# Forming the convolved half of a Mamba block's input projection directly as channels x time

## The reference

```python
xz = layernorm(x) @ in_proj_w.T          # 512 -> 2048
xi, z = split(xz, 2)                     # 1024 each
xt = conv1d(transpose(xi), conv_w, 4 taps, causal, per channel) + conv_b
xc = silu(transpose(xt))                 # 1024 channels
xp = xc @ x_proj_w.T                     # dt, B, C  (33 columns)
delta = softplus(xp[..., 0:1] * dt_w + dt_b)
# for each of 16 states s: A_bar, chunked cumulative sums over 128 steps,
# y = sum_s C_s * h_s + D * xc
x = x + (y * silu(z)) @ out_proj_w.T
x = x + int8-like product of layernorm(x) with L0_ffn_rhs
```

## Time and profile before

| | |
|---|---|
| timed runs | 5839.98, 5842.17, 5845.01 us (median 5842.17) |
| the profiled execution: from its first to its last instruction | 5836.6 us (no time of its own is listed beside this span) |
| PE busy | 5616.2 us, 96% |
| DVE busy | 5351.4 us, 92% |
| ACT busy | 3734.7 us, 64% |
| POOL busy | 2457.2 us, 42% |
| granted TensorE clock, mean | 0.992 of 2.4 GHz |

### The profile page before, as it was taken

The page is one execution under the profiler, slowest core; times in us unless marked ns, Lnnn a source line. Parts: engine busy times, 40 slices in busy tenths (PEclk is TensorE's granted clock), DMA queues, the critical chain, the costliest instruction groups (busy, mean ns, idle before and its releaser), DMA issues. The chain is left out here.

```text
span 5836.6 us, 78230 instructions
## 1 busy us (share of the span) xinstructions
PE 5616.2 (96%) x16088; PEld 2643.7 (45%) x16152; DVE 5351.4 (92%) x7057; ACT 3734.7 (64%) x4618; POOL 2457.2 (42%) x2139
## 2 busy tenths in 40 slices
PE   5999999999999999999999999999999999999998
PEld 2444444444444444444444444444444444444443
DVE  4999999999999999999999999999999999999997
ACT  3666666666666666666666666666666666666664
POOL 2444444444444444444444444444444444444443
PEclk9999999999999999999999999999999999999999
DMA  1122121121121211212212112112122121121220
GB/s 68 12 18 20 15 18 16 15 20 16 15 19 14 18 17 15 20 16 15 20 14 17 17 17 18 16 15 20 14 17 19 14 18 16 15 20 16 15 18 12
DMA packets 157893, 104.23 MB, mean 18 GB/s; under 512 B 121008, under 2 KB 121008, under 8 KB 157488
## 3 DMA queue, kind: packets, MB, share of 16 engines
q1 hardware_dynamic: 157488, 100.71, 19.0%
HBM read 42.63 MB, written 16.78 MB: 10 GB/s over the span
## 5 line engine op out<-in xcount | busy, mean ns | idle before, releaser
L487 POOL TENSOR_SCALAR room<-total,limit 128x1024 f32<-128x1024 f32 x1024 | 1183.1, 1155 | 3245.6 <-PE cum L1038 475.3
L739 ACT ACTIVATE decay<-cum,neg_a 128x1024 f32<-128x1024 f32 x1024 | 1137.3, 1111 | 1543.0 <-PE cum L1038 1539.3
L1048 PE MATMUL state<-sources,tri_upto 128*128 128x512 f32 x4096 | 1971.5, 604 | 123.9 <-DVE term L1380 123.5
L1038 PE MATMUL cum<-step,tri_before 128*128 128x512 f32 x4096 | 1938.8, 596 | 3.5 <-DVE sources L1367 3.5
L1380 DVE SCALAR_TENSOR_TENSOR term<-state,crow,decay 128x1024 f32<-128x1024 f32 x1024 | 1312.6, 1282 | 312.9 <-PE state L1048 196.0
L1390 DVE TENSOR_TENSOR acc<-acc,term 128x1024 f32<-128x1024 f32 x1024 | 1359.2, 1327 | 0.2
L1367 DVE SCALAR_TENSOR_TENSOR sources<-cum,brow,dx 128x1024 f32<-128x1024 f32 x1024 | 1305.5, 1275 | 10.0 <-ACT cum L755 10.0
L1038 PEld LDWEIGHTS cum<-step,tri_before 128*128 128x128 f32 x4096 | 781.1, 192 | 966.3 <-issue 943.7
L755 ACT ACTIVATE cum<-room,pos_a 128x1024 f32<-128x1024 f32 x1024 | 1143.6, 1117 | 110.6 <-POOL room L487 101.8
L1048 PEld LDWEIGHTS state<-sources,tri_upto 128*128 128x128 f32 x4096 | 743.3, 190 | 994.3 <-issue 867.3
L476 POOL TENSOR_SCALAR step<-delta,limit 128x1024 f32<-128x1024 f32 x1024 | 1144.7, 1118 | 8.3 <-PE cum L1038 7.0
(11 more groups left out here) (127 smaller groups left out, 3630.5 us busy)
## 6 DMA issues: line engine op xcount, KB each, us to landing
hfirst<-hrows SPq DMA_DIRECT2D x496, 64.0 KB, 3.9
xt<-in_x SPq DMA_DIRECT2D x64, 256.0 KB, 2.6
hrows<-term SPq DMA_DIRECT2D x1024, 4.0 KB, 1.6
xres<-in_x SPq DMA_DIRECT2D x64, 256.0 KB, 2.7
out_x<-xres SPq DMA_DIRECT2D x64, 256.0 KB, 2.1
gate_last<-gate SPq DMA_DIRECT2D x512, 0.5 KB, 2.0
win<-in_w_in SPq DMA_DIRECT2D x2, 2048.0 KB, 10.8
hrows<-hrows SPq DMA_DIRECT2D x64, 64.0 KB, 2.3
```

Of the source, the lines that this page charges most:

```text
L487: nc.gpsimd.tensor_scalar(room[:, :], total[:, :], limit[:, s:s + 1], 0.0, ALU.min, ALU.max).then_inc(limited, 1)
L739: nc.scalar.activation(decay[s % 4][:, :], cum[s % 2][:, :], ACT.Exp, scale=neg_a[:, s:s + 1]).then_inc(decay_ready, 1)
L1038: last = nc.tensor.matmul(cum[s % 2][:, cols], tri_before[:, :], step[s % 2][:, cols], start=True, stop=True)
L1048: last = nc.tensor.matmul(state[:, cols], tri_upto[:, :], source[s % 2][:, cols], start=True, stop=True)
```

## The change

The 1024 channels of `xi` are formed at once with channels on the partitions: a block of `win` (128 x 128) becomes the weights and `xnT` is streamed, 128 columns, over four blocks of the contraction. One half is 4 channel blocks x 4 = 16 matmuls of 128 columns, issued in two parts of eight. The steps `xi0` and `xi1` leave PE's and ACT's lists, and so do the two copies into `xi`, the eight transposes, and three waits of `front_xi`, of which the one on `carry_merged` moves to `front_abs`. On PE the first half of the channels stands in slot 15 (first part) and slot 0 (second part), the second half in slots 2 and 3. On ACT the copies to `xiT` and the fourth taps move from slots 3 and 4 to slots 1 and 3.

```diff
-FRONT_ACT = ("xi0", "xi1", "xiT0", "tap3a", "xiT1", "tap3b", "z0", ...
+FRONT_ACT = ("xiT0", "tap3a", "xiT1", "tap3b", "z0", ...
-FRONT_PE = ("xi0", "xi1", "xiT0", "xiT1", "z0", ...
+FRONT_PE = ("xiT0", "xiT1", "z0", ...
...
             def front_abs(t):
                 act.wait_ge(front_dve, at(FRONT_DVE, t, "dt_lin"))
+                if t.shift(-2) is not None:
+                    act.wait_ge(carry_merged, t.n - 1)
...
@@ ACT body
-                        if s == 0:
-                            front_xi(nxt, 0)
-                        if s == 2:
-                            front_xi(nxt, 1)
-                        if s in (3, 4):
-                            front_xiT(nxt, s - 3)
+                        if s in (1, 3):
+                            front_xiT(nxt, s // 2)
...
-                        if s in (3, 4):
-                            front_tap3(nxt, s - 3)
+                        if s in (1, 3):
+                            front_tap3(nxt, s // 2)
...
@@ PE
-            def front_xiT(t, h):
-                front_free(t, f"xiT{h}")
-                turn4(lambda j: xi[:, (4 * h + j) * P:(4 * h + j + 1) * P]).then_inc(front_pe, 1)
+            def front_xiT(t, h, part):
+                if part == 0:
+                    pe.wait_ge(norm_act, at(NORM_ACT, t, "xnT"))
+                    front_free(t, f"xiT{h}")
+                for j in (2 * part, 2 * part + 1):
+                    block = slice((4 * h + j) * P, (4 * h + j + 1) * P)
+                    for k in range(KD):
+                        last = nc.tensor.matmul(fbank[:, j * P:(j + 1) * P], win[:, k, block], xnT[t.parity][:, k, :],
+                                                start=(k == 0), stop=(k == KD - 1))
+                if part == 1:
+                    last.then_inc(front_pe, 1)
...
@@ PE body
                         if s == 0:
-                            front_in(nxt, "xi0", 0, 1)
-                        if s in (1, 2):
-                            front_in(nxt, "xi1", HALF, s - 1)
-                        if s in (3, 4):
-                            front_xiT(nxt, s - 3)
+                            front_xiT(nxt, 0, 1)
+                        if s in (2, 3):
+                            front_xiT(nxt, 1, s - 2)
...
                     if more2 and s == 15:
-                        front_in(t.shift(2), "xi0", 0, 0)
+                        front_xiT(t.shift(2), 0, 0)
```

More of the change, by code:

```diff
@@ L52 @@
              "log1p", "delta", "dx")
-FRONT_ACT = ("xi0", "xi1", "xiT0", "tap3a", "xiT1", "tap3b", "z0", "xcT", "proj", "xc0", "abs", "exp", "over", "xc1",
+FRONT_ACT = ("xiT0", "tap3a", "xiT1", "tap3b", "z0", "xcT", "proj", "xc0", "abs", "exp", "over", "xc1",
              "square", "ln", "z1", "total0", "total1", "ct")
-FRONT_PE = ("xi0", "xi1", "xiT0", "xiT1", "z0", "proj", "xc0", "xc1", "z1", "total0", "total1", "ct")
+FRONT_PE = ("xiT0", "xiT1", "z0", "proj", "xc0", "xc1", "z1", "total0", "total1", "ct")
 FRONT_POOL = ("skip",)
@@ L606, in evacuate @@
                 nc.scalar.activation(dst, src, func).then_inc(front_act, 1)
[L608 to L615, removed]
             def front_xiT(t, h):
@@ L771, in start @@
                 norm_xnT(t)
-                front_xi(t, 0)
-                front_xi(t, 1)
                 front_xiT(t, 0)
@@ L1075, in start @@
                 for h in range(2):
[L1076 to L1079, removed]
+                    front_xiT(t, h, 0)
+                    front_xiT(t, h, 1)
                 front_in(t, "z0", DI, 0)
@@ L1090, in start @@
                 norm_xnT(t.shift(1))
-                front_in(t.shift(1), "xi0", 0, 0)
+                front_xiT(t.shift(1), 0, 0)
                 cumulate(t, 0)
```

## The result

The kernel after takes **6006.4 us** (median, 6005.9 to 6007.2) where the kernel before takes 5842.2 (5840.0 to 5845.0): a ratio of 1.028, 95% interval 1.027 to 1.030. It is slower by 164 us; 57 were forecast, and the range ended at 5940. The profiled execution spans 6004.0 us, 167.4 more than that of before.

What follows compares the result with a forecast made beforehand. PE was taken to bind in some slots and DVE in others; 33.5 + 25.0 + 0.5 = 59 us over 62 tiles, less 2 at the start, gave +57, span 5893.6, plus 5.6 for the median: 5899 us, range 5875 to 5940.

Steps and rivals of the forecast that it cites:

- the price of a part: On PE, eight new 128-column matmuls (16 records) cost 1.81 us, 0.113 us a record, weight loads overlapping the stream.
- the rival in which they don't: On PE, weight loads add to the stream: parts of 3.50 us, 210 us more than forecast, some 6110 us; chance 0.04.
- the rule of the Trainium skill: Weight loads overlap running matmuls only in another row group; here, no overlap, so a PE part costs the sum, 3.50 us.
- the path through slots 1 to 3: On PE: slot 1 gains at most 0.31 us, slot 2 grows by 0.11 us, slot 3 by 1.28 us, delaying term 3.
- Slot 3 at 7.28 us: PE's slot 3 exchanges four turns (0.53 us) for a 1.81 us part, growing 1.28 us while still holding hT.
- state 1 bound to term 0: PE's state 1 can't start sooner than 1.43 us after DVE's term 0, because there is one state buffer.
- 15.94 and 16.01 us from term 0 to term 3: DVE's distance in a pair's second and first tiles, up 1.08 and 1.39 us.
- the late first tiles: At 13 pair boundaries with halved clock, slot 1's freed time absorbs a 1.35 us wait, leaving +0.04 us a tile.
- DVE's idle before term 3: DVE's wait for PE's state 3 grows from 0.80 us to near 2 us.
- slots 15 and 0 "at nothing": PE's slots 15 and 0 exchange 1.70 for 1.81 us, costed at nothing because PE waits 2.46 us for DVE there.
- the clock's rival: Emptied slot 1 idles PE, so its clock falls more often: up to 1.7 us each, 53 us, 5952 us; chance 0.14.
- PE's busy time: Over the whole kernel, PE's busy time falls by some 30 us while its wait for DVE's term grows more.

Runs made afterwards that it cites:

- Experiment 2: Kernel after, with PE's never-taken branch for a carry between chunks emptied, shortening PE's loop to about 1356 instructions: 5895.9 us, ratio 1.009.
- 5: Kernel before, with PE's never-taken branch for a carry between chunks emptied, as a control: 5838.4 us, ratio 0.999.
- experiment 1: Kernel before, with only PE's loop head placed at instruction 180 of a 256-instruction block: 5942.9 us, ratio 1.017.
- 9: Kernel before, with only PE's loop head placed at slot 0 of a 256-instruction block: 5842.4 us, ratio 1.000.
- 12: Kernel before, with only PE's loop head placed at slot 100 of a 256-instruction block: 5843.1 us, ratio 1.000.
- 11: Kernel after, with the second half's parts in PE's slots 1 and 2, PE's carry branch as a hardware loop, prefetch hint on DVE's loop: 5745.5 us, ratio 0.983.
- experiment 8: Kernel before, with the prefetch hint on DVE's loop alone: 5773.6 us, ratio 0.988.
- 7: Kernel after, with the second half's parts in PE's slots 1 and 2 and the prefetch hint on PE's and DVE's loops: 5964.3 us, ratio 1.020.
- 3: Kernel after, with the second half's parts in PE's slots 1 and 2 and ACT's copies in slots 0 and 2: 5957.1 us, ratio 1.019.

## Why the prediction was right in its slots and wrong in its sum

- **Right: the price of a part.** 1.81 us were taken from L944, 1.78 were measured, 0.111 us a record with its weight load. The loads hide; the rival in which they don't falls, and with it the rule of the Trainium skill beside it, as the prediction reads it.
- **Right: the path through slots 1 to 3.** Slot 3 at 7.28 us (measured 7.20), state 1 bound to term 0 (1.43 us behind it, as in the earlier trace rows), 15.94 and 16.01 us from term 0 to term 3 (16.04 in every tile), the late first tiles swallowed by the emptied slot 1. DVE's idle before term 3, forecast near 2 us, is 1.56, with 0.49 more before the reading of hT. Experiment 2 against 5 gives 57.5 us for all of it. That it fits to half a microsecond is luck: second tiles cost 1.18 us (forecast 1.08), first ones 0.78 on the mean (forecast 0.82).
- **Wrong: slots 15 and 0 "at nothing".** The step exchanged 1.70 for 1.81 us and named the 2.46 us that PE waits there for DVE as cover. The cover is real for work: with the code loaded, in experiment 2, term 0 follows term 15 by 6.22 us, as before. But the step counted microseconds and not instructions. PE's loop grew by 156 of them, ceased to stay loaded, and PE stood 2.24 + 1.71 + 1.96 = 5.91 us at the turn shown, far beyond the cover. The missing term is 28 x 3.73 = 104 us; by experiments 2 and 1 it is 110 and 98.
- **Where it could have been read.** The third part of the page of before has 25 packets on queue 8 and 380 on queue 14: of the two engines one was loaded and one not. The prediction never read it. That the loop of before ended just into its eighth block could be counted from the program; that a further 70 instructions would be too many could not be read from any row, and only 1, 9 and 12 show it.
- **Half right: the clock's rival.** The clock does fall more often (half-clock time 178 us instead of 93). Where no fetch is behind it, in experiment 2 (150 us), it costs next to nothing. In the kernel after it falls behind PE's stops at the turn, before state 0, and there it does reach the path, for 1.74 us a fall by experiment 1. The rival had the size (up to 1.7 us), but put the fall down to the emptied slot 1.
- **Wrong: PE's busy time.** Forecast 30 us lower, it is 14.6 higher (5630.8 against 5616.2): records at half clock take about twice as long, and 178 us stood at half in place of 93. Where the clock stays up, in 11, it is 5560.4.

## What to carry to other kernels

Count a change in instructions as well as in microseconds: here a loop body near the room that PE has for code lost a hundred microseconds to 156 more instructions, or to a move without any, and code that never runs took up that room too. Read the instruction queues on the page before costing an edit: here 25 packets went with a loop that stays loaded, and 280, nine for each round, with one that pays at each turn. When a part is moved, give it to the slot where another engine binds, and look at what that slot was making up for.

## What the runs showed of the hardware that was not expected

- The same 1707 instructions take 5842 or 5943 us by the place of the loop's head alone (heads at 0 and 100 against 180).
- A fetch on PE's path shows as idle "issue" or "PEq", of 1.71 to 2.24 us each at the turn shown: three of them, with four packets on the queue.
- Before, the wait ahead of term 15 at a turn is put down to ACT's decay, 89.9 us in all on DVE's term; experiment 8 takes most of it away with a hint on DVE's loop alone, so it was DVE's own code. That hint is worth 70 us in a kernel whose PE loop is loaded (8), and together with PE's nothing in one whose PE loop is not (7 is no faster than 3).
